# An expert layer on one core: down weights split once for all experts, down products in three split products, SiLU by one activation

## The reference

```
scores = xn @ gate_w.T                      # 8 experts
topk_scores, topk_idx = top_k(scores, 2)
topk_probs = softmax(topk_scores)
h1, h2 = split(xn @ w12[e].T)               # 512 + 512 per expert
hidden = silu(h1) * h2
y = sum over the two experts of  topk_probs * (hidden @ w3[e].T)
out = x + attention(xn) + y
```

## Time and profile before

| what | value |
|---|---|
| median of 3 runs | 734.41 us (734.2 to 734.74) |
| the profiled execution | 735.36 us |
| its span, first to last instruction | 733.6 us |
| PE busy | 659.0 us (90%) |
| DVE busy | 571.9 us (78%) |
| ACT busy | 520.9 us (71%) |
| expert phase, first `tokens` to the restart of the attention | 158.0 to 535.8 us |

### The profile page before, as it was taken

One profiled execution on the slowest core, in us unless ns is written; L12 is line 12 of the kernel. 1 busy time (PEld: TensorE's weight loads), 2 busy tenths in 40 slices (PEclk: granted clock), 3 DMA queues, 4 the chain that ended last, 5 costly groups with the idle time before them and its releaser, 6 DMA issues.

```text
span 733.6 us, 17179 instructions
## 1 busy us (share of the span) xinstructions
PE 659.0 (90%) x5648; PEld 522.4 (71%) x5649; DVE 571.9 (78%) x908; ACT 520.9 (71%) x880; POOL 346.3 (47%) x330
## 2 busy tenths in 40 slices
PE   0876786979999999999999999999989898989995
PEld 0654564758888888888888888888867676767674
DVE  4859899867777777777777777777867879797884
ACT  4545486556777777777777777777757787988885
POOL 3000471113656565656565656665511335566654
PEclk9999898979999999999999999999999999999999
DMA  8893677560111111111111111111147697875840
GB/s 293 274 274 129 162 268 269 147 233 29 50 50 50 50 50 50 50 50 50 50 50 50 50 50 50 50 50 50 50 122 217 181 264 188 269 204 180 218 148 29
DMA packets 66351, 92.56 MB, mean 126 GB/s; under 512 B 6432, under 2 KB 53408, under 8 KB 66304
## 3 DMA queue, kind: packets, MB, share of 16 engines
q1 hardware_dynamic: 57872, 70.40, 32.1%
q0 software_dynamic: 6864, 18.75, 7.9%
q10 hardware_dynamic: 1568, 2.76, 1.2%
HBM read 59.06 MB, written 32.83 MB: 125 GB/s over the span
## 4 chain that ended last, share of the span: by engine, by line
PE 65%; DVE 14%; ACT 9%; issue 7%; DMA 2%; POOL 2%; DVEq 0%; ACTq 0%; SPq 0%; POOLq 0%
PE PS L1226 58%; PE PS L1472 4%; DVE SMALL L912 4%; ACT WORK L762 3%; DVE XN L1071 2%; PE PS L1450 2%; DVE WALL L906 2%; ACT QS L757 2%; DMA XN<-in_x 1%; DVE WORK L981 1%; DVE WORK L974 1%; DMA KS<-parts_scratch 1%; ACT WORK L700 1%; DVE WALL L930 1%; ACT SIDE L769 1%
## 5 line engine op out<-in xcount | busy, mean ns | idle before, releaser
L1226 PE MATMUL PS<-WS,XTS 128*128 128x512 f32 x852 | 243.0, 421 | 1.9 <-DVE XTS L906 1.5
L349 DVE TENSOR_TENSOR WS<-WALL,WS 128x1024 fp32r<-128x1024 f32 x144 | 176.4, 1225 | 83.9 <-ACT WS L838 83.1
L838 ACT ACTIVATE WS<-WALL 128x1024 fp32r x144 | 152.2, 1059 | 57.9 <-issue 55.4
L1226 PEld LDWEIGHTS PS<-WS,XTS 128*128 128x128 f32 x852 | 157.1, 191 | 32.3 <-DVE XTS L906 1.9
L1226 PE MATMUL PS<-WALL,WORK 128*128 x568 | 136.7, 384 | 0.8 <-ACT WORK L854 0.8
L635 POOL DMA_INDIRECT WORK<-xn_scratch,GIDX x72 | 120.2, 1669 | 24.7 <-issue 21.6
L576 POOL TENSOR_TENSOR OTS<-SIDE,XN 128x256 f32<-128x256 f32 x31 | 23.5, 759 | 209.2 <-DVE XN L1071 142.0
L1226 PEld LDWEIGHTS PS<-WALL,WORK 128*128 128x128 f32 x568 | 102.2, 190 | 13.4 <-issue 1.0
L912 DVE TENSOR_REDUCE SMALL<-PS 128x8 f32<-128x1024 f32 x64 | 77.5, 1211 | 13.0 <-PE PS L1226 12.7
L762 ACT ACTIVATE WORK<-PS 128x512 f32<-128x512 f32 x128 | 69.4, 595 | 23.4 <-PE PS L1226 20.3
L639 POOL DMA_INDIRECT ys_scratch<-OTS,SIDX x35 | 54.7, 1562 | 63.4 <-ACT OTS L864 63.4
(11 more groups left out here) (139 smaller groups left out, 988.6 us busy)
## 6 DMA issues: line engine op xcount, KB each, us to landing
WALL<-in_wexp SPq DMA_DIRECT2D x28, 384.0 KB
WALL<-ys_scratch SPq DMA_DIRECT2D x16, 512.0 KB, 7.1
parts_scratch<-WORK SPq DMA_DIRECT2D x32, 240.0 KB, 2.4
QS<-parts_scratch SPq DMA_DIRECT2D x16, 480.0 KB, 4.5
XN<-in_x SPq DMA_DIRECT2D x4, 1024.0 KB, 12.7
xn_scratch<-XN SPq DMA_DIRECT2D x4, 1024.0 KB, 7.7
WALL<-in_x SPq DMA_DIRECT2D x8, 512.0 KB, 5.7
KS<-parts_scratch SPq DMA_DIRECT2D x16, 240.0 KB, 4.0
```

The lines of the kernel that those rows point to most:

```text
L349: eng.tensor_tensor(out=WS[:, 1 - k, half, 1], in0=weights, in1=WS[:, 1 - k, half, 0].bitcast(F32), op=ALU.subtract).then_inc(low_ready[ha ...
L838: act.activation(WS[:, 1 - k, half, 0], weights, ACT.Copy).then_inc(high_ready[half], 1)
L1226: return pe.matmul(o, a, b, start=start, stop=stop)
```

## The change

- Down products: DOWN_HIGH (float32r, a new region that takes the stacks' second halves after batch 1) and DOWN_LOW (in the place of the down weights in WALL) hold all 8 experts' down weights as high and low part. They are made once, before the first down product: 2 highs by DVE, 6 by ACT, 8 lows by DVE. `down` becomes 12 float32r products of 128x256. The hidden values are split per tile: `take_ht` writes the high part, a new `low_ht` on DVE the low part.
- The first 4 tiles (EXACT_UP) use plain float32 up products straight from WALL, without splitting up weights or x.
- SiLU: `take_silu` by one activation function in place of tanh on ACT and `gated` on DVE; the factor 0.5 goes from the shares. The function's table is loaded by a small activation (`bring_table`) ahead of the phase, and the table of Exp again at its end, and once ahead of the first exps.
- The order in the loop: PE turn_hidden(j), up(j+1, 0), up(j+1, 1), tokens(j+2), down(j). ACT take_ht(j), high_part(j+2, 0), take_silu(j+1), high_part(j+2, 1), take_xt(j+2), take_y(j). DVE low_ht(j), low_part(j+2, 0), hidden(j+1), low_xt(j+2), low_part(j+2, 1). The loop now begins at tile 4.
- The weights' loads have two semaphores (`weights_in` for experts 0 to 5, `late_in` for 6 and 7). XS has a buffer of its own. The scratch region for DMA descriptors is set to 2048 bytes for each partition. One small DMA restores constant rows of KS after the phase (`hot_back`).

```diff
+EXACT_UP = 4
+DOWN_ORDER = (3, 4, 0, 1, 2, 5, 6, 7)
+DOWN_AT = (0, 1, 4, 6, 8)
+BY_DVE_ALONE = 2
...
+            bring_table(ACT.Exp)
             take_shift(0, 0)
...
+                bring_table(ACT.Silu)
                 act.wait_ge(temps_done, 1)
-                act.wait_ge(weights_in, 16 * E * CHUNKS)
+                act.wait_ge(weights_in, 16 * LATE * CHUNKS)
...
-                    act.activation(HID[:, k, :], bank(2 * k), ACT.Tanh, scale=0.5).then_inc(tanh_ready, 1)
+                    act.activation(HID[:, k, :], bank(2 * k), ACT.Silu).then_inc(silu_ready, 1)
...
+                def high_down(n):
+                    e = DOWN_ORDER[n]
+                    if e >= LATE:
+                        act.wait_ge(late_in, 16 * (E - LATE) * CHUNKS)
+                    act.activation(DOWN_HIGH[:, e], WALL[:, e * WE + WU:(e + 1) * WE], ACT.Copy
+                                   ).then_inc(highs_made, 1)
+                high_down(2)
+                take_exact_xt(0, 0)
+                take_exact_xt(1, 1)
+                high_down(3)
+                take_silu(0, 0)
+                for n in range(4, E):
+                    high_down(n)
...
+                with act.Fori(EXACT_UP // 2, SLOT_TILES // 2) as i:
                     for k in range(2):
-                        tile(2 * i + k, k, i)
+                        j = 2 * i + k
+                        take_ht(j)
+                        high_part(j + 2, k, 0, j + 1)
+                        take_silu(j + 1, 1 - k)
+                        high_part(j + 2, k, 1, j + 1)
+                        take_xt(j + 2, k)
+                        take_y(j, k, i)
                 last = SLOT_TILES - 1
                 take_ht(last)
                 take_y(last, last % 2, last // 2)
+                bring_table(ACT.Exp)
...
+            def low_down(n):
+                e = DOWN_ORDER[n]
+                if n < BY_DVE_ALONE:
+                    dve.wait_ge(weights_in, 16 * LATE * CHUNKS)
+                    link(dve.tensor_copy(DOWN_HIGH[:, e], WALL[:, e * WE + WU:(e + 1) * WE]))
+                else:
+                    dve.wait_ge(highs_made, n + 1 - BY_DVE_ALONE)
+                tt(DOWN_LOW[:, e * WE:e * WE + WD], WALL[:, e * WE + WU:(e + 1) * WE], DOWN_HIGH[:, e].bitcast(F32), ALU.subtract).then_inc(lows_made, 1)
...
+                def low_ht(j):
+                    dve.wait_ge(ht_high, j + 1)
+                    tt(HTS[:, 1], bank(6).rearrange("p (c n) -> p c n", c=FC), HTS[:, 0].bitcast(F32),
+                       ALU.subtract).then_inc(ht_free, 1)
+                for n in range(*DOWN_AT[1:3]):
+                    low_down(n)
                 hidden(0, 0)
+                for n in range(*DOWN_AT[2:4]):
+                    low_down(n)
+                low_ht(0)
+                for n in range(*DOWN_AT[3:5]):
+                    low_down(n)
...
                     for f in range(FC):
-                        last = mm(bank(7)[:, 0:D], HTS[:, f, :],
-                                  WALL[:, bass.ds(at + 2 * NC_D * FH + f * D, D)], f == 0, f == FC - 1)
+                        high = high_parts[:, bass.ds(e * WD + f * D, D)]
+                        for part, of in ((0, high), (1, high), (0, DOWN_LOW[:, bass.ds(e * WE + f * D, D)])):
+                            last = mm(bank(7)[:, 0:D], HTS[:, part, f, :], of, n == 0, n == 3 * FC - 1)
+                            n += 1
...
+                for j in range(EXACT_UP):
+                    k = j % 2
+                    if j:
+                        turn_hidden(j, k)
+                    if j + 1 < EXACT_UP:
+                        ahead = expert(j + 1)
+                        exact_up(j + 1, 1 - k, 0, ahead)
+                        if j == 0:
+                            turn_hidden(j, k)
+                        exact_up(j + 1, 1 - k, 1, ahead)
+                    else:
+                        up(j + 1, 1 - k, 0)
+                        up(j + 1, 1 - k, 1)
+                    tokens(j + 2, k)
+                    if j == 0:
+                        pe.wait_ge(lows_made, E)
+                    down(j, expert(j))
+                with pe.Fori(EXACT_UP // 2, SLOT_TILES // 2) as i:
                     for k in range(2):
                         j = 2 * i + k
+                        turn_hidden(j, k)
                         up(j + 1, 1 - k, 0)
-                        at = expert(j)
-                        turn_hidden(j, k)
+                        e = expert(j)
                         up(j + 1, 1 - k, 1)
                         tokens(j + 2, k)
-                        down(j, at)
+                        down(j, e)
```

More of the change, by code:

```diff
@@ L477, in _ @@
             sp.wait_ge(y_stored, 1)
+            sp.dma_start(KS[STK:DEEP, 1], KS[STK:DEEP, 0]).then_inc(hot_back, 16)
             def send_later(n, b):
@@ L1172, in batch @@
                         invert()
+                        for n in range(*DOWN_AT[0:2]):
+                            low_down(n)
                     project(b, NWIN - 1)
@@ L1182, in _ @@
                     break
-                low_part(dve, 0, 0, 0)
                 dve.wait_ge(r_free, c["R"].now() + 1)
[L1186 to L1189, removed]
                 def hidden(j, k):
-                    dve.wait_ge(g_done, j + 3)
+                    dve.wait_ge(silu_ready, j + 3)
                     dve.wait_ge(h2_full, j + 1)
@@ L1196, in low_xt @@
                 def low_xt(j, k):
-                    dve.wait_ge(xt_high, j + 1)
+                    dve.wait_ge(xt_high, j + 1 - EXACT_UP)
                     tt(XTS[:, k, 1], bank(4 + k)[:, 0:D].rearrange("p (c n) -> p c n", c=NC_D),
                        XTS[:, k, 0].bitcast(F32), ALU.subtract).then_inc(xt_free, 1)
[L1201 to L1205, removed]
-                hidden(0, 0)
-                low_part(dve, 1, 1, 1)
-                with dve.Fori(0, SLOT_TILES // 2) as i:
+                def low_ht(j):
[4 more added lines that the diff above has]
+                    low_down(n)
+                hidden(0, 0)
+                for n in range(*DOWN_AT[2:4]):
+                    low_down(n)
+                low_ht(0)
+                for n in range(*DOWN_AT[3:5]):
+                    low_down(n)
+                for j in range(EXACT_UP):
+                    k = j % 2
+                    if j:
+                        low_ht(j)
+                    if j + 2 >= EXACT_UP:
+                        low_part(dve, j + 2, k, 0)
+                    hidden(j + 1, 1 - k)
+                    if j + 2 >= EXACT_UP:
+                        low_xt(j + 2, k)
+                        low_part(dve, j + 2, k, 1)
+                with dve.Fori(EXACT_UP // 2, SLOT_TILES // 2) as i:
                     for k in range(2):
                         j = 2 * i + k
+                        low_ht(j)
                         low_part(dve, j + 2, k, 0)
-                        gated(j + 1, 1 - k)
+                        hidden(j + 1, 1 - k)
                         low_xt(j + 2, k)
-                        hidden(j + 1, 1 - k)
                         low_part(dve, j + 2, k, 1)
-                dve.wait_ge(low_ready[1], XS_TILES)
+                low_ht(SLOT_TILES - 1)
+                dve.wait_ge(low_ready[1], XS_TILES - EXACT_UP)
                 dve.sem_inc(phase_done, 1)
@@ L1412, in batch @@
                     elif not last:
+                        if b == EXTRA:
+                            pe.wait_ge(hot_back, 16)
                         shifted(1 - par, 0)
@@ L1473, in turn_hidden, with exact_up @@
                     last.then_inc(ht_full, 1)
-                def down(j, at):
+                def exact_up(j, k, half, e):
+                    full, free = ((h1_full, silu_ready), (h2_full, hid_done))[half]
+                    if half == 0:
+                        pe.wait_ge(xt_free, j + 3)
+                    pe.wait_ge(free, j + 1)
+                    for ch in range(NC_D):
+                        last = mm(bank(2 * k + half), EXACT_XTS[:, k, ch],
+                                  WALL[:, bass.ds(e * WE + (2 * ch + half) * FH, FH)], ch == 0, ch == NC_D - 1)
+                    last.then_inc(full, 1)
```

104 lines of the change are left out of this document (63 added, 41 removed).

## The result

The changed kernel takes 713.9 us (713.24 to 714.79, 4 runs) against 734.3 beside it: a ratio of 0.9727, interval 0.9715 to 0.9739. The forecast was 724 with 719 to 731 as its own range. The direction was right and the gain, 20.4 us, twice what was forecast; the time lies 0.1 us under the wide range (714 to 738). Single executions that ran at a low clock throughout (one of run 10, one of run 11, one of the kernel before beside them) are left out of every median and ratio here.

What follows compares the result with a forecast made beforehand. PE bounds the loop: 5.222 to 5.00 us a tile over 66 tiles saves 14.7, start costs 2.7, end 1.8, so -10.2 from 735.36: 725.2, median 724. Own range 719 to 731, wide range 714 to 738.

Steps and rivals of the forecast that it cites:

- The rival in which ACT takes over: Loop: with p 0.107 to 0.12, ACT holds the period near 4.87 to 4.93, 715 to 720 us; chance 0.20.
- p: Pitch in us of the new 256-column float32r down matmuls: bounds 0.107 and 0.19, taken as 0.125, test range 0.12 to 0.135.
- The float32r surcharge: Up product: float32r pitch 0.2325 against 0.215 for a plain matmul, so 0.0175 was added to the down matmul's 0.107.
- The rest of PE's sum: PE's tile apart from the down product: up 2.79, transpositions 0.66, lost between kinds 0.05; with down 1.50, 5.00 us.
- the end: Last turn_hidden to attention's restart: 5.7 us against 3.9, costing 1.8, with the Exp table load of 1.28 in the path.
- the start: From the phase's beginning to the loop at tile 4: reached at 189.8 in place of 187.1, costing 2.7 us.
- The pair of matmuls 0.13 apart: Two matmuls of only 32 columns, read as the pace of a 128-column load behind a started matmul, supporting 0.125.
- The rival of loads that pace the product: The 12 loads of down: weight loads set a pitch over 0.138; at 0.145 740 us, at 0.19 776; chance 0.15.
- The chain of ACT: Loop, take_ht to low_xt, ending at 5.18: bounds the period at 4.72, or 4.95 with the branch, under 5.00.
- As before, 4.23: DVE's work per tile: gated (0.68) goes, low_ht (0.68) comes, so the sum stays 4.23 us.
- the ring: Loop, chain of hidden values: turn_hidden(j+1) waits for hidden(j+1), ready at 4.6, before 5.0, with 0.4 to spare.
- R3: ACT's order: a register load of 0.66 behind SiLU too gives period 5.1 to 5.2, 728 to 736 us; chance 0.16.

Runs made afterwards that it cites:

- run 10: Kernel before with both SiLU by one function (no gated) and the new loop order, down products still plain: 733.2 us, ratio 0.9981.
- run 11: Changed kernel with plain up products in 2 tiles, not 4, two more high down parts ahead of the first SiLU, and DVE's lows reordered: 708.5 us.
- run 1: Kernel before with only the new loop order on PE, ACT and DVE, tanh and gated kept: 736.8 us, ratio 1.0031.
- run 4: Changed kernel with each of the 12 down products over 384 columns in place of 256, for timing alone: 764.0 us.
- run 6: Changed kernel with plain float32 down products, no split down weights and no low_ht: 732.1 us, ratio 0.9971 to the kernel before.
- run 3: Changed kernel with each of the 12 down products over 128 columns in place of 256, leaving out half the expert results: 713.1 us.
- run 9: Kernel before with SiLU by one function on ACT and no gated on DVE, all else as before: 734.7 us, ratio 1.0003.
- run 5: Changed kernel with the old loop order on PE and ACT, and low_ht behind the first low part on DVE: 778.5 us, ratio 1.0599.
- run 2: Changed kernel with tanh on ACT and gated ahead of hidden on DVE again, all else as changed: 741.4 us, ratio 1.0103.
- run 8: Changed kernel with two more high down parts on ACT ahead of the first SiLU, and DVE's lows reordered around hidden(0) and low_ht(0): 709.4 us.

## Why the prediction came out at half the gain

- **PE is the bound, before and after.** Right, though the reading it rested on, 50.00 of 50 us, was not enough for it (run 1); the periods of runs 4 and 6 are. The rival in which ACT takes over fell, though p came out in its range: ACT waits for PE 0.9 us a tile ahead of take_y.
- **The step that failed: p = 0.107 + 0.0175 = 0.125.** Measured 0.1144, outside the 0.12 to 0.135 which the prediction itself had set as its test. The float32r surcharge was read at 512 columns and added to 256 as if it belonged to the instruction. Runs 3 and 4 show that it belongs to the column. By rate, 0.2325 / 2 = 0.116 stood in the rows that I had. The term: 12 x (0.125 - 0.1144) x 66 = 8.4 us of the 11.9 us between the forecast's change of span (10.2) and the measured one (22.1). The rest of PE's sum gives 2.1, the end 1.5, the start -0.2. The pair of matmuls 0.13 apart seemed to confirm 0.125. It is a first matmul and its successor, not a pace; run 3 has the pace, 0.112.
- **The rest of PE's sum.** Apart from p the sum was 0.03 a tile too high, 2.1 us. The 0.05 lost between kinds was carried over from the old order, and the new order loses about as much less as is missing: run 10 against run 9, 5.19 against 5.22.
- **The rival of loads that pace the product** has its mechanism (run 3) but its price is 0.112, not over 0.138, and at 256 columns the stream costs no less. The load's shown duration of 0.19 is in all runs, at pitches down to 0.112.
- **The chain of ACT was put too long.** I carried the 0.27 of the register load ahead of each high part into the new order. Behind SiLU it is gone:

```profile
302.76 1.06 ACT L862 ACTIVATE WS<-WALL 128x1024 fp32r x1
303.72 0.58 ACT L873 ACTIVATE WORK<-PS 128x512 f32<-128x512 f32 x1
304.20 1.05 ACT L862 ACTIVATE WS<-WALL 128x1024 fp32r x1
```

  The second high part starts 0.48 after SiLU. In the order of before, it stood behind take_xt, which had waited for PE. The order decides: from 200 to 500 us the runs in the old order have such gaps (run 9 44.7 us ahead of 115 high parts, run 5 40.5 us ahead of 104), and runs 1 and 10, the kernel before in the new order with tanh or SiLU, have none that the waits show. That the load is hidden because nothing ahead of it waits fits all of these; it was not tested by itself.
- **SiLU and gated.** "As before, 4.23" was right for the sum and missed what the function does: it takes 0.7 us out of the ring. Alone it is worth nothing (run 9), in the changed kernel 27.5 us (run 2). The order alone costs 2.3 (run 1), the old order with the split 65 (run 5). So the three parts are one change, with the reservation on run 5 that the place of low_ht on DVE wasn't tuned.
- **The start.** 2.7 forecast, 2.9 measured, in part by luck. PE's first plain up product began 0.6 earlier than forecast and lost 1.3 us to the low clock in place of 2.9, so PE stood at the first down product from 167.65 and not from 169.7. The lows were there at 171.2 in place of 172.0. The wait was 3.5 in place of 2.4, and the lower clock that the forecast had only ahead of it came back behind it: 1.1 us more in the down product and 0.4 in the transpositions after it.
- **Sums that don't come out.** By the prediction's own terms R3's periods of 5.1 to 5.2 give 731 to 737 where it says 728 to 736, and p from 0.12 to 0.135 gives 720 to 732 where it says 719 to 731. Neither decides anything.
- **The end.** 1.8 forecast, 0.3 measured. The table load isn't in the path:

```profile
513.28 0.38 ACT L893 ACTIVATE SIDE<-PS 128x256 f32<-128x256 f32 x1 [2.53 <-PE PS L1300]
513.68 1.28 ACT L840 ACT_TABLE_LOAD   x1
513.75 1.34 PE L1300 MATMUL PS<-WORK,WQKV 128*128 128x320 f32 x4 [0.51 <-ACTq L943]
```

  PE restarts at 513.75, 0.07 after the load began: in this trace ACT's addition to `phase_done` did not wait for the load queued ahead of it. The forecast had put 1.48 us for the load and the small activation into the path; without them it is 0.3. ACT's next work comes at 515.22, 1.47 after PE's restart; before it was 1.46 (535.84 and 537.30). The Trainium skill (ScalarE: Activation LUTs, What ACT_TABLE_LOAD costs) gives 1.28 for the load, as here, and 1.38 of drain on top. Here the small activation follows at 514.98, 0.02 after the load.

## What to carry to other kernels

When a shape is missing from the trace, take its price once as a constant and once as a rate from the nearest shape, and forecast between the two; here the rate was right and the constant was worth 8 us over 800 products. On a loop whose bound is one engine, relieving another gives nothing by itself, but look for the ring that ties one tile to the next: its slack decides which other parts of a change may be made. Where the bound engine waits for a preparation that is made once, count the wait and also what the engine's clock loses behind it, and look for idle time of the engine that makes the preparation: run 8 filled such idle time and got both back. A busy share of 100% doesn't prove a bound; lengthening the engine's own work and watching the period does.

## What the runs showed of the hardware that was not expected

A float32r matmul with its own load of 128 columns starts 0.112, 0.1144, 0.173 and 0.2325 us after the one before at 128, 256, 384 and 512 columns, full clock.

PE that stood for 3.51 us did its next 12 products at the lower clock level, in 2.58 us; after 1.45 us of standing (run 8) they took 1.47. The window of 170 to 180 us has a granted clock of 0.83 in the first case and 1.00 in the second. The length of standing alone doesn't decide it: at the end of the phase PE stands for 1.50 us in the changed kernel and keeps its clock, and for 1.51 us in run 3, with half the columns in its down products, where it falls to the lower level 0.6 us after taking up work again.

POOL's indirect gathers show 1.71 us each in the loop before and with SiLU alone (run 9), 0.97 with the new order on the same buffers (runs 1 and 10), and 1.04 with the old order in the changed kernel (run 5). So the new order is enough to shorten them, but not needed. What the gathers collide with in the kernel before was not looked for, since POOL bounds nothing here.
